# Preparing layer 1 of a two-layer kernel inside the last attention head of layer 0, with an earlier first q load and a reordered opening

## The reference

```
x = x + L0(gn(x))     # gn: group norm, 32 groups
x = x + L1(gn(x))
L0: qkv = depthwise3x3(W_qkv . x + b) ; q, k normalized over the head's 48 channels
    attn = softmax(temperature * q^T k), 4 heads, 4096 x 4096 scores each ; out = W_proj . (v attn^T) + b
L1: xn = layernorm over channels ; Q, K, V = Wq xn, Wk xn, Wv xn ; S = Q^T K (one head, 192 channels)
    attn = e1/(e1+e2) softmax(S) + e2/(e1+e2) relu(S)^2 ; out = attn V + x
```

## Time and profile before

| | |
|---|---|
| median of 3 runs | 3410.62 us (3407.66 to 3412.9) |
| profiled execution | 3413.54 us, its span 3411.8 us |
| PE busy | 3197.9 us, 94% of the span |
| ACT, DVE, POOL busy | 2204.5, 1903.0, 934.1 us |
| last product of layer 0 read by DVE | 1944.69 us |
| last statistics of layer 1, image 0, begin | 2003.76 us |
| first score of image 0, image 1 of layer 1 | 2120.49, 2841.18 us |

### The profile page before, as it was taken

How to read it: one execution, slowest core, us unless ns; L and a number is a source line. 1 busy time by engine, 2 the same in 40 slices (tenths; PEclk the granted TensorE clock), 3 DMA queues, 4 the chain that set the end, 5 groups by cost and what they waited for, 6 DMA issues and landing times. The chain is left out here.

```text
span 3411.8 us, 47896 instructions
## 1 busy us (share of the span) xinstructions
PE 3197.9 (94%) x16354; PEld 1276.1 (37%) x16354; DVE 1903.0 (56%) x2461; ACT 2204.5 (65%) x2428; POOL 934.1 (27%) x485
## 2 busy tenths in 40 slices
PE   3799999999999999999999778999999787999998
PEld 1222222322223222222222234555555344555555
DVE  6551347431553525375111165888888555888886
ACT  5256556566555665565666524988888256888886
POOL 1002021020020210210200001666666213666665
PEclk7799999999999999999999979999999888999999
DMA  5312113111132021210200042677777824777777
GB/s 151 85 33 61 46 34 72 45 38 50 32 84 54 14 60 43 60 49 26 58 11 10 18 121 81 123 143 144 143 144 143 142 90 100 143 142 142 142 142 134
DMA packets 685382, 286.20 MB, mean 84 GB/s; under 512 B 602416, under 2 KB 644144, under 8 KB 682608
## 3 DMA queue, kind: packets, MB, share of 16 engines
q1 hardware_dynamic: 680400, 275.65, 38.0%
q10 hardware_dynamic: 4800, 8.26, 1.1%
HBM read 85.99 MB, written 34.21 MB: 35 GB/s over the span
## 5 line engine op out<-in xcount | busy, mean ns | idle before, releaser
L437 ACT ACTIVATE prob<-ps_s,cur 128x1024 f32<-128x1024 f32 x1024 | 1085.4, 1111 | 723.1 <-PE ps_s L652 722.0
L665 PE MATMUL ps_a<-prob,vt 128*64 128x512 f32 x4096 | 993.3, 606 | 0.0
L1623 PE MATMUL ps_s<-kst,qs 128*128 128x512 f16 x2560 | 640.4, 383 | 29.4 <-DMA qs<-q_scratch 18.8
L1319 POOL TENSOR_TENSOR p_lo<-gp,p_hi 128x1024 f16<-128x1024 f32 x256 | 550.6, 2161 | 399.6 <-ACT p_hi L1453 394.5
L1636 PE MATMUL ps_o<-v_hl,at_hi 128*128 128x384 f16 x2048 | 548.6, 329 | 33.6 <-DMA at_lo<-p_lo 33.3
L646 PE MATMUL ps_s<-q_a,k_a 128*128 128x512 f16 x2048 | 534.7, 383 | 4.2 <-issue 2.2
L1636 PE MATMUL ps_o<-v_hl,at_lo 128*128 128x192 f16 x2048 | 505.5, 248 | 0.0
L665 PEld LDWEIGHTS ps_a<-prob,vt 128*64 128x64 f32 x4096 | 248.7, 136 | 409.7 <-issue 409.0
L1890 DVE TENSOR_SCALAR_CACHE_REDUCE neg<-ps_s,mix 128x1024 f32<-128x1024 f32 x256 | 327.3, 1278 | 132.5 <-PE ps_s L1623 131.3
L1623 PEld LDWEIGHTS ps_s<-kst,qs 128*128 128x128 f16 x2560 | 245.1, 99 | 257.1 <-issue 31.4
L646 PEld LDWEIGHTS ps_s<-q_a,k_a 128*128 128x128 f16 x2048 | 132.5, 97 | 543.4 <-ACT prob L437 471.4
(11 more groups left out here) (226 smaller groups left out, 2728.9 us busy)
## 6 DMA issues: line engine op xcount, KB each, us to landing
z<-z_scratch SPq DMA_DIRECT2D x80, 384.0 KB, 3.8
sq<-rn_scratch SPq DMA_DIRECT2D x14, 768.0 KB, 10.8
qs<-q_scratch SPq DMA_DIRECT2D x64, 128.0 KB, 2.8
rden<-den_scratch SPq DMA_DIRECT2D x64, 96.0 KB, 2.2
o_scratch<-o_s SPq DMA_DIRECT2D x64, 96.0 KB, 1.9
res_scratch<-xg SPq DMA_DIRECT2D x4, 1536.0 KB, 7.3
q_scratch<-qst SPq DMA_DIRECT2D x32, 192.0 KB, 2.4
res<-res_scratch SPq DMA_DIRECT2D x64, 96.0 KB, 2.2
```

Of the source, the lines that this page charges most:

```text
L437: act.activation(prob[:, a % PR, :], ps_s[:, a % 2, :], ACT.Exp, bias=cur[:, slot:slot + 1], scale=1.0 / SPLIT).then_inc(exped, 1)
L665: ins = pe.matmul(ps_a[h * HALF:(h + 1) * HALF, j % 2, :], vt[:, slot, m, :], prob[:, a % PR, h * CH:(h + 1) * CH], start=(m == 0), stop=( ...
L1319: pool.tensor_tensor(p_lo[:, cols], prob[s][:, cols], p_hi[:, cols], ALU.subtract).then_inc(lo_made[c], 1)
L1623: ins = pe.matmul(ps_s[:, c % 2, h * CH:(h + 1) * CH], qs[:, s, qt, :], kst[:, ktile, cols], start=(t == 0), stop=(t == len(terms) - 1))
```

## The change

1. Nine weight loads and the sixteen loads of o and x are issued by SP during the last head, into memory that layer 0 no longer uses; layer 1 keeps these tiles.
2. The small PE products go into the last head's hook: the product of Wq and Wk at block 1, step 8 (`fuse_weights`), the others at block 2, step 0 (`reach_weights`). DVE's chain up to them (`prepare_weights`) stands behind `finish` of block 1, the one behind them (`fit_weights`) behind `finish` of block 2.
3. The projection of image 0 (`project_ahead`) stands on PE right behind the last product. `residual_ahead` 0 and 1 stand on DVE ahead of the last `finish`, the others behind it.
4. In each prologue SP loads q rows 0 and 1 behind chunk 4's transfers, not behind all of them, and the first score waits for one evacuation less.
5. On ACT two of the four `add_normed` stand behind the first root, and a one-element root ahead of them brings its function table in early.
6. In the opening three evacuations of v's projection stand on ACT ahead of image 1's normalization; half of the `k_b` DMAs go from ACT's queue to SP's; four of the eight v transposes and evacuations stand between the last pieces of convolution.

```diff
+                def reach_weights():
+                    pe.wait_ge(a_reach, REACH)
+                    pe.wait_ge(a_set, 2)
...
                 def odd(i, last):
                     def prep(j, m, uses):
+                        if last and j == 1 and m == 8:
+                            fuse_weights()
+                        if last and j == 2 and m == 0:
+                            reach_weights()
                         if last:
                             return
...
                     copy_acc(g, 1)
                     finish(g, 1)
+                    if last:
+                        prepare_weights()
...
                     finish(g, 2)
+                    if last:
+                        fit_weights()
...
                     copy_acc(g, 3)
+                    if last:
+                        residual_ahead(0)
+                        residual_ahead(1)
                     finish(g, 3)
+                    if last:
+                        for c in range(2, NCH):
+                            residual_ahead(c)
...
+                    for c in range(NCH):
+                        place_k(c)
+                        if c >= 2:
+                            store_q(c - 2)
+                        if c == 4:
+                            sp.wait_ge(q_out[0], 4 * 16 * (NCH // 2 * b + 1))
+                            load_q(0, 0, True)
+                            load_q(1, 1, True)
...
-                                pe.wait_ge(s_free, b * PRO + 2 + PRO)
+                                pe.wait_ge(s_free, b * PRO + 2 + PRO - 1 + c)
...
-                pe.wait_ge(conv_op, CONV_OPS * 2)
+                pe.wait_ge(conv_op, CONV_OPS + TAPS)
                 for q in range(8):
+                    if q == FAR - 1:
+                        pe.wait_ge(conv_op, CONV_OPS * 2)
...
                     conv_half(1, vv, 1, 1, 18, range(1 + 2 * c, 3 + 2 * c), ROWS)
-                dve.wait_ge(vt_set, 2)
-                for q in range(8):
+                    evac_vt(c, uses.next())
+                for q in range(4, 8):
                     evac_vt(q, uses.next())
```

More of the change, by code:

```diff
@@ L522, in _ @@
                 evac_sums(0)
+                act.wait_ge(w_in[1], 48)
+                for c in range(3):
+                    evac_project(1, c, 9)
                 act.wait_ge(gn1_pow, 3)
@@ L554, in _ @@
                     head(0, 2 * i + 2)
-                head(1, 2 * PAIRS - 1)
+                head(1, 2 * PAIRS - 1, True)
             @block.tensor
@@ new lines, in project_ahead @@
+                def project_ahead(c):
+                    pe.wait_ge(a_loaded, 32 * NCH)
+                    if c < 2:
+                        pe.wait_ge(exped, STEPS * B * HEADS + 2)
+                    else:
+                        pe.wait_ge(a_sum, 2 * (c - 2) + 1)
+                    for o in range(CT):
+                        for t in range(CT):
+                            ins = pe.matmul(ps_s[0:CP, c % 2, o * CH:(o + 1) * CH], a["wp"][:, t, o * CP:(o + 1) * CP],
+                                            a_o[:, c, t, :], start=(t == 0), stop=(t == CT - 1))
+                    ins.then_inc(a_product, 1)
@@ L720, in _ @@
                 odd(PAIRS - 1, True)
+                for c in range(NCH):
+                    project_ahead(c)
             @block.vector
@@ L1048, in layer1 @@
         MORE = C - P
+        with ExitStack() as first:
+            sb("below_sq", [CP, 2, CT, N], F32, first)
+            sq_buf = sb("sq_buf", [CP, 2, CT, CH], F32, first)
+        kst = sb("kst", [P, RT, N], F16)
+        with ExitStack() as second:
+            below_xs = sb("below_xs", [CP, CT, 2 * CH], F32, second)
+            xs = sb("xs", [CP, 2, 2, CT, CH], F16, second)
+            qst = sb("qst", [CP, 2, 2, CT, CH], F16, second)
+        at_hi = sb("at_hi", [P, 2, KT, P], F16)
+        at_lo = sb("at_lo", [P, 2, KT, P], F16)
+        p_hi = sb("p_hi", [P, N], F16)
+        p_lo = sb("p_lo", [P, N], F16)
+        qs = sb("qs", [P, 2, QT, P], F16)
+        res = sb("res", [CP, 2, CT, P])
+        ot = sb("ot", [CP, 2, CT, P])
+        ahead_buffers(lambda name, shape: sb("kept_" + name, shape))
+        xg, wqk, wv, wp, pvec, mix = a["xg"], a["wqk"], a["wv"], a["wp"], a["pvec"], a["mix"]
+        group, meanm, ident, stats, mhalf = a["group"], a["meanm"], a["ident"], a["stats"], a["half"]
+        unscale, top = a["unscale"], a["top"]
         gp = sb("gp", [P, CT, N])
@@ L1555, in pair_free @@
                         return (n[0] - 1) % 2
-                    if not b:
-                        for c in range(NCH):
-                            project(b, c)
                     for j, src in enumerate((0, 2)):
@@ L1788, in stat_step @@
                         dve.wait_ge(stat, st[0])
-                    if not b:
-                        for c in range(NCH):
-                            residual(b, c)
-                            if 3 <= c < 7:
-                                fit_weights(c - 3)
                     for t in range(CT):
```

390 lines of the change are left out of this document (194 added, 196 removed).

## The result

| | before | after |
|---|---|---|
| median of 4 runs (range), us | 3410.66 (3407.66 to 3412.9) | 3388.32 (3385.89 to 3390.32) |
| ratio, 95% interval | | 0.9932 [0.9918, 0.9946] |
| profiled execution, its span | 3413.54, 3411.8 | 3385.89, 3384.1 |
| last copy of layer 0 to the first `bn_aggr` | 60.38 | 32.56 |

The changed kernel is 22.3 us faster by the medians.

What follows compares the result with a forecast made beforehand. PE was taken to set the pace in layer 0's heads, a chain of waits elsewhere. 19.8 - 26.9 - 12.1 + 3.1 - 3.7 = -19.8 us gives 3393.7 profiled, 3391 median; own range 3384 to 3398, widened to 3378 to 3403.

Steps and rivals of the forecast that it cites:

- opening: Before the first head: three earlier ACT evacuations and early v transposes save 3.7 us; first head at about 141.6, not 145.26.
- wait for DVE's chain in the last head: Last head, block 2: PE stands still in `reach_weights` until DVE's chain behind block 1's `finish` ends, costing 12.35 us.
- fuse, reach, low clock: Last head: added products of `fuse_weights` (1.5 us) and `reach_weights` (2.4), plus low clock after PE's pause (3.5).
- between the layers: Last copy of layer 0 to the last statistics: PE projects at once, ending at 1978.1 instead of 2005.04, 26.9 us saved.
- prologues up to the last low part of q (ACT's order): Both prologues: an `add_normed` ahead of the second square delays it and PE's chain by 1.5 us, 3.1 for both images.
- from there to the first scores: Both prologues: with q rows 0 and 1 loaded early the first score no longer waits for the load, 12.1 us saved.
- The rival that the wait isn't there: Last head: DVE's chain is ready in time, so PE does not wait; 3375 us, chance 0.07.
- The clock behind it: Last head, behind PE's wait: a low-clock stretch of 4.2 to 10 us loses half of itself, taken as 3.5 us.
- The rival of a stuck clock: Last head: the clock stays low after the pause and the kernel gets slower; 3484 us at half clock throughout, chance 0.03.
- the break: Between the layers: PE waits 1.6 us ahead of projection chunk 4 for residual 2's first half, behind DVE's `finish`.
- the change of programs: Between the layers: the program change falls on the path, costing 0 to 3.1 us, taken as 1.0.
- the early transposes: End of the opening: with four v pieces already done only the fifth's own 1.2 us is left, a gain of 3.4.

Runs made afterwards that it cites:

- The filled wait: Changed kernel with 15, then 19, unread filling products on PE ahead of the wait in `reach_weights`: 3385.99 us (ratio 0.9924) and 3385.75 us (0.9923).
- the twelve edits: The follow-up kernels, all edits of the changed kernel (products, fillers, q loads, ACT's order, root, opening, `finish`, combinations); measured from 3368.05 to 3404.01 us.

## Why the prediction was right, step by step

It said 3391, and the median is 3388.3, a gain of 22.3 where 19.6 was forecast. From profile to profile the gain is 27.7, where the terms added up to 19.8. Each term against the trace (profile to profile, us):

| step | forecast | measured |
|---|---|---|
| opening | -3.7 | -4.8 |
| heads 0 to 6 | 0 | -1.3 |
| wait for DVE's chain in the last head | +12.35 | +12.07 |
| fuse, reach, low clock | +7.4 | +7.7 |
| between the layers | -26.9 | -27.8 |
| prologues up to the last low part of q (ACT's order) | +3.1 | +3.0, of which 2.8 by the comparison at the same clock |
| from there to the first scores | -12.1 | -12.1 |
| rows behind the first scores | 0 | -4.4, of which 2.6 low clock at the score |
| sum | -19.8 | -27.7 |

- **The wait in the last head** was right in place, cause and size. `finish` of block 1 plus the chain, counted from the copy, against one turn of PE, was enough. The rival that the wait isn't there fell. Moving the products 12 steps later removed it.
- **The clock behind it** was right as a cost (3.5 forecast). The filled wait shows 3.5 (69.36 - 65.85), and that PE's pause is the cause. The rival of a stuck clock did not come: the clock was low until 1862.9, and a normal turn began at 1864.5. The case of over 50 us which the Trainium skill tells of ("TensorE: Matmul & The Clock Gate", section "Seeing it yourself") was seen in no run here; the longest low stretch in the changed kernel's trace lasts 31 us, in the opening.
- **Between the layers** the break was 1.33 us (forecast 1.6) and the change of programs 0.73 (forecast 1.0). The bounds of that term used 1953.99, the end of the last `finish` in the kernel before, which the earlier trace rows does not show:

```profile
1953.30 0.69 DVE L826 TENSOR_TENSOR o_s<-acc_s,rden 128x512 f32<-128x512 f32 x1
```

- That DVE's order with `finish` decides the break is shown from both sides, 3.73 and none. No run undoes the early loads or the early products between the layers, so the 27.8 as a whole rests on the rows: PE projects right behind its last product, where before 18.1 us of idle time and the first small products stood between the earlier trace rows.
- **The first scores**: the waits were exact. The step that priced only the wait missed its second part. Both late first scores ran at half clock for 3.8 to 4.2 us; of the early ones that of image 0 did for 2.8 us and that of image 1 not at all. That is 2.6 us. The earlier trace rows had shown the low clock behind the old first score; I used it for the last head's price and not here. The other 1.8 of the 4.4 lie within what one kernel's rows vary by, and nothing here tells them from chance.
- **The opening** came out near its forecast for the wrong reason. The step that failed is "ACT issues two DMAs fewer for each, so I let the convolution end where it did". ACT's issue was the pace of those parts, and its relief is worth 3.7 us. Of the 3.4 that I gave the early transposes 1.8 came at the end, since the transfer of q_b then held the first score, and their first evacuation took 1.9 back by its stop of 6.07 us. I had named this stall and set it against idle time. The last 1.1 of the 4.8 lie ahead of the first high part; eight kernels with this opening begin at 141.5 on average, so about 1 us of the 4.8 is luck of this profile.
- **ACT's order** went the forecast way, in size too: 1.4 us a prologue against 1.5, with no slack behind it. A single pair of profiles hides it, by when the clock rises.
- **Heads 0 to 6**: from the first score to the last copy of head 6 the kernel before takes 1598.03 us and the changed one 1596.71, but the twelve edits, which leave these heads alone, take 1596.5 to 1598.7. The 1.3 us are no effect of the change that these traces can show.
- **The range.** With every term at its bound the sum gives 3383 to 3401; the own range of 3384 to 3398 takes it that they don't all fall to one side. No reading above depends on it.

## What to carry to other kernels

When a product that waits is put into a saturated TensorE stream, count when its input is ready from the same event as the stream's own position; if it is later, put the product that many steps further on, which here took 15.8 us off the block. Price every pause of TensorE at the clock behind it as well: in these runs pauses of 2.22, 3.73 and 12.07 us each cost 3.1 to 3.5 us on top, so half-closing a gap gains little and closing it gains all. An engine that issues DMAs between its operations is held by them (two of ACT's took 1.2 to 1.5 us), so look at its issue rows and its "issue" idle time before believing that it has room. And before two profiles are compared at a place where TensorE comes back from a pause, compare when the clock rose in each.

## What was not expected of the hardware

A pause of 2.22 us, ahead of which PE had been busy without a gap, was enough to find the clock at 1.2 GHz, and it stayed there some 6.8 us, nearly as long as behind a pause of 12.07 us (7.7 us from the restart). A break of 1.33 us did nothing. Between the two lies no fixed limit that these traces show. Ahead of a first score PE paused 1.90 us in the run with ACT's order undone (image 1, score at 2817.92) and 1.89 us in the run with k_b on ACT (image 0, 2107.80), behind the same products with the clock at 1.00. Here are the stretches behind the two scores:

```profile
2818.00:2820.00 2.00, 2.00 (x8) 0.72 0.58 167
```

```profile
2108.00:2110.00 2.00, 2.00 (x11) 1.00 0.61 176
```

In the first the clock fell, about 1 us after PE had restarted; in the second it stayed up. The time from PE's restart to full clock varied from 3.7 to 7.0 us at one and the same place of the program. Such a spread in one profile is as large as the effects looked for here. Only the same row over many kernels, or a comparison at the same clock, tells them apart.
